# A two-layer convolution kernel: the ScalarE order of the filter pass changed, and the statistics of its output taken on ScalarE by sums of value and square instead of by VectorE's batch-norm instructions

## What is computed

```
# layer 0: four levels; level i works on x pooled by 2**i
y = relu(conv3x3(pool(x, 2**i), ds_w3[i], dilation d_i)); y = conv1x1(y, ds_w1[i])
# attention on each level: the first 16 channels
ker = gelu(mean(f_att) @ kg_w1.T + kg_b1) @ kg_w2.T + kg_b2      # one 3x3 kernel per image and channel
out = conv1x1(concat(conv13x13(f_att) + depthwise3x3(f_att, ker), f_idt))
x   = x + conv1x1(sum over levels of the upsampled outputs)
# layer 1: the group norm needs mean and variance of the x that layer 0 gave
x   = x + sum over ten branches of (5x5 convolution, nine shifts of a 3x3 convolution) of group_norm(x)
```

## Time and profile before

| what | value |
| --- | --- |
| median of 3 runs | 3051.51 us (3051.09 to 3056.02) |
| the profiled execution's own time | 3052.12 us |
| its span in the profile | 3050.3 us |
| TensorE matmuls busy in the span | 2688.6 us (88%) |
| VectorE busy | 2153.3 us (71%) |
| ScalarE busy | 992.0 us (33%) |
| GpSimd busy | 645.2 us (21%) |

### The profile page before, as it was taken

One profiled execution on the slowest core, in us unless ns is written; L12 is line 12 of the kernel. 1 busy time (PEld: TensorE's weight loads), 2 busy tenths in 40 slices (PEclk: granted clock), 3 DMA queues, 4 the chain that ended last, 5 costly groups with the idle time before them and its releaser, 6 DMA issues. The chain is left out here.

```text
span 3050.3 us, 39267 instructions
## 1 busy us (share of the span) xinstructions
PE 2688.6 (88%) x12262; PEld 2153.5 (71%) x12262; DVE 2153.3 (71%) x3003; ACT 992.0 (33%) x1606; POOL 645.2 (21%) x732
## 2 busy tenths in 40 slices
PE   0499999996999699999999688888994999999998
PEld 0366776664788678888888566777773777777776
DVE  7444444433345488888888778888876999999998
ACT  1011111110111077778777422222211333232332
POOL 5444433331222143443344200000001000000000
PEclk9999999998889699999999799999996999999999
DMA  4422222210000299999998313333344223333332
GB/s 75 100 71 70 65 71 64 65 42 16 8 13 15 39 199 212 218 215 214 212 217 208 112 59 140 143 127 127 129 151 161 88 88 117 92 113 97 109 103 69
DMA packets 288699, 337.99 MB, mean 111 GB/s; under 512 B 24816, under 2 KB 243824, under 8 KB 274288
## 3 DMA queue, kind: packets, MB, share of 16 engines
q1 hardware_dynamic: 285072, 336.15, 41.2%
q10 hardware_dynamic: 3552, 0.89, 0.1%
HBM read 211.60 MB, written 122.62 MB: 110 GB/s over the span
## 5 line engine op out<-in xcount | busy, mean ns | idle before, releaser
L373 PE MATMUL ps_all<-vh,u_h 128*128 128x512 f32 x960 | 384.7, 401 | 28.7 <-DVE vl L2633 27.8
L375 PE MATMUL ps_all<-vh,u_l 128*128 128x512 f32 x960 | 383.3, 399 | 0.0
L374 PE MATMUL ps_all<-vl,u_h 128*128 128x512 f32 x960 | 382.9, 399 | 0.0
L2542 ACT ACTIVATE vh<-rt,gn 128x528 fp32r<-128x528 f32 x192 | 130.4, 727 | 445.9 <-DVE rt L2610 331.2
L373 PE MATMUL ps_all<-vh,t_h 128*128 128x512 f32 x576 | 231.2, 401 | 22.3 <-DVE vl L1691 22.3
L373 PEld LDWEIGHTS ps_all<-vh,u_h 128*128 128x128 f32 x960 | 180.9, 188 | 82.3 <-issue 35.7
L375 PE MATMUL ps_all<-vh,t_l 128*128 128x512 f32 x576 | 229.7, 399 | 0.0
L374 PE MATMUL ps_all<-vl,t_h 128*128 128x512 f32 x576 | 229.4, 398 | 0.0
L375 PEld LDWEIGHTS ps_all<-vh,u_l 128*128 128x128 f32 x960 | 181.0, 189 | 46.2
L374 PEld LDWEIGHTS ps_all<-vl,u_h 128*128 128x128 f32 x960 | 181.1, 189 | 45.5
L373 PE MATMUL ps_all<-nh,w3h 128*128 128x512 f32 (+1 forms) x396 | 161.0, 407 | 32.3 <-POOL nl L1078 24.5
(11 more groups left out here) (384 smaller groups left out, 6688.6 us busy)
## 6 DMA issues: line engine op xcount, KB each, us to landing
xc<-in_x SPq DMA_DIRECT2D x128, 256.0 KB, 3.8
xr<-in_x SPq DMA_DIRECT2D x128, 256.0 KB, 4.2
x_layer<-xr SPq DMA_DIRECT2D x64, 512.0 KB, 2.7
xq<-x_layer SPq DMA_DIRECT2D x32, 1024.0 KB, 4.8
x_layer<-xq SPq DMA_DIRECT2D x32, 1024.0 KB, 3.8
out<-ot SPq DMA_DIRECT2D x64, 512.0 KB, 5.2
xw<-in_x SPq DMA_DIRECT2D x112, 288.0 KB, 5.0
xw<-x_layer SPq DMA_DIRECT2D x16, 1152.0 KB, 8.7
```

Of the source, the lines that this page charges most:

```text
L373: pe.matmul(o, wh, xh, start=first, stop=False, skip_group_check=True)
L374: pe.matmul(o, wh, xl, start=False, stop=False, skip_group_check=True)
L375: return pe.matmul(o, wl, xh, start=False, stop=last, skip_group_check=True)
L2542: act.activation(vh[:, v % 2, n, :, :].rearrange("p a b -> p (a b)"), rt[:, n, :, :].rearrange("p a b -> p (a b)"), ACT.Identity, scale=gn ...
```

## The change

In the convolution pass ScalarE gets one more activation per tile, `low_phases`, which lays out the low part for the phases 0 and 1 in a new buffer `rp_l`; the products for `dc` 2 and 3 read their low part there, without a step. It waits for VectorE's `r_low`; TensorE waits for it ahead of the third product. The added pads of `rp_l` are two more memsets on GpSimd, once.

In the filter pass `bn_stats` is gone from `add_attention`. ScalarE's new `moments(a, c)` has four activations of 1024 elements per partition per chunk: for each half of the chunk a sum of the values and a sum of the squares of value minus the image's earlier mean, written to a scratch area (`void`, in the place of the weights `kg2`) that nothing reads; each waits for the one before it. `collect` becomes six small VectorE operations in a row in place of one. The copy of bank 0 for t = 2 stood first in the next period; it now stands in the image's own period, ahead of `high_dynamic(n, 2)`. SyncE's `store_x` waits for the chunk's moments before it lets the buffer be loaded again.

```diff
 # convolution pass, ScalarE
+                    def low_phases(i, t):
+                        n = NT * i + t
+                        act.wait_ge(r_l, 1 + n + 1)
+                        v = rl[:, t % 2, :, 2:2 + W].bitcast(F32).rearrange("p n (q d) -> p n q d", d=4)[:, :, :, 0:2]
+                        act.activation(rp_l[:, t % 2, :, :, 1:33].rearrange("p d n q -> p n q d"), v,
+                                       ACT.Identity).then_inc(r_p, 1)
...
                                 high_phases(*later(i, t, 1))
+                                low_phases(*later(i, t, 1))
                             features(i, t)
 # convolution pass, TensorE
                         for dc in range(4):
+                            if dc == 2:
+                                pe.wait_ge(r_p, n + 1)
...
+                            low = rl[u] if dc < 2 else rp_l[v]
                             mm = product(pe, ps_fa[:, 0:272].rearrange("p (n q) -> p n q", q=34), fa_h[:, dc, :],
-                                         fa_l[:, dc, :], rp_h[v], rl[u], dc == 0, dc == 3)
+                                         fa_l[:, dc, :], rp_h[v], low, dc == 0, dc == 3)
 # filter pass, SyncE, store_x
                         sp.wait_ge(x_st, 16 * (4 * a + c + 1))
                         alone(sp)
+                        sp.wait_ge(bn, 4 * (4 * a + c + 1))
+                        alone(sp)
 # filter pass, ScalarE
+                    def moments(a, c):
+                        act.wait_ge(qfree, 4 + 16 * a + 4 * c + 4)
+                        for h in range(2):
+                            v = xq[:, c % 2, 8 * h:8 * h + 8, :].rearrange("p a b -> p (a b)")
+                            k = 2 * c + h
+                            act.wait_ge(bn, 16 * a + 2 * k)
+                            act.activation(void, v, ACT.Identity, accum_out=sx[:, k:k + 1]).then_inc(bn, 1)
+                            act.wait_ge(bn, 16 * a + 2 * k + 1)
+                            alone(act)
+                            act.activation(void, v, ACT.Square, bias=nm0[:, bass.ds(a, 1)],
+                                           accum_out=sq[:, k:k + 1]).then_inc(bn, 1)
...
                     def period(i, a, s, n):
                         first = i is None
-                        if a is not None:
-                            copy(a, 2)
                         if i is not None:
                             high(i, 8, isinstance(i, int) and i == 0)
...
                             high_lk(a, 1)
+                            moments(a, 0)
...
                             high_lk(a, 3)
+                            moments(a, 1)
                         if i is not None:
                             copy(i, 1)
                         if n is not None:
                             high_dynamic(n, 1, first)
                             high(n, 6, first)
+                        if a is not None:
+                            moments(a, 2)
+                        if n is not None:
                             high(n, 7, first)
+                        if i is not None:
+                            copy(i, 2)
+                        if n is not None:
                             high_dynamic(n, 2, first)
+                        if a is not None:
+                            moments(a, 3)
 # filter pass, VectorE
-                        for e in range(4):
-                            dve.bn_stats(stat[:, 4 * c + e, :], xq[:, c % 2, 4 * e:4 * e + 4, :].rearrange(
-                                "p a b -> p (a b)")).then_inc(bn, 1)
...
-                        stats.done(dve.bn_aggr(mv, stat[:, :, :].rearrange("p a b -> p (a b)")))
+                        mo.done(dve.tensor_reduce(tx, sx[:, :], AX.X, ALU.add))
+                        mo.done(dve.tensor_reduce(tq, sq[:, :], AX.X, ALU.add))
+                        mo.wait(dve)
+                        mo.done(dve.tensor_scalar(mv[:, 0:1], tx, one, None, ALU.mult))
+                        mo.wait(dve)
+                        alone(dve)
+                        mo.done(dve.tensor_tensor(dd, mv[:, 0:1], nm0[:, bass.ds(s, 1)], ALU.add))
+                        mo.wait(dve)
+                        alone(dve)
+                        mo.done(dve.tensor_tensor(dd, dd, dd, ALU.mult))
+                        mo.wait(dve)
+                        stats.done(dve.scalar_tensor_tensor(mv[:, 1:2], tq, one, dd, ALU.mult, ALU.subtract))
```

More of the change, by code:

```diff
@@ L132, in conv_kernel @@
         kb1 = mb("kb1", [ATT // 2, 1])
-        kg2 = mb("kg2", [ATT // 2, 9, P])
+        kg2a = mb("kg2", [P, 9, P])
+        kg2 = kg2a[0:ATT // 2, :, :]
         kb2 = mb("kb2", [P, 9])
@@ L1438, in conv_kernel @@
             rp_h = sb("rp_h", [P, 2, 4, 8, 36], F32R, stack=st)
+            rp_l = sb("rp_l", [P, 2, 2, 8, 36], F32R, stack=st)
             ft = sb("ft", [P, 4, NPAIR, 9], stack=st)
@@ L1450, in conv_kernel @@
             main, m_c, y_d = sa("main"), sa("m_c"), sa("y_d")
-            r_f, r_h, r_l = sa("r_f"), sa("r_h"), sa("r_l")
+            r_f, r_h, r_l, r_p = sa("r_f"), sa("r_h"), sa("r_l"), sa("r_p")
             q_f, q_x = sa("q_f"), sa("q_x")
@@ L1458, in conv_kernel @@
             w_t3 = Steps(sa("w_t3"), 10)
-            NT3, NFA, NPD = 7, 13, 8
+            NT3, NFA, NPD = 7, 13, 10
             def later(i, t, k):
@@ L1550, in pads @@
                             pool.memset(t[:, :, :, 0:W + 2:W + 1].bitcast(F32), 0.0).then_inc(w_z, 1)
-                        for t in (rp_h,):
+                        for t in (rp_h, rp_l):
                             v = t[:, :, :, :, :].rearrange("p s d n q -> p (s d n) q").bitcast(F32)
@@ L1666, in _ @@
                     high_phases(0, 0)
+                    low_phases(0, 0)
                     with act.Fori(0, B - 1) as i:
@@ L1850, in conv_kernel @@
             ms = sb("ms", [P, 2], stack=st)
+            nm0 = sb("nm0", [P, B], stack=st)
+            sx = sb("sx", [P, 8], stack=st)
+            sq = sb("sq", [P, 8], stack=st)
+            void = kg2a[:, :, :].rearrange("p a b -> p (a b)")[:, 0:8 * W]
+            mo = Steps(sl("mo"), 5)
+            nm_s = sl("nm_s")
             b_p, b_w, b_h, b_g = sl("b_p"), sl("b_w"), sl("b_h"), Steps(sl("b_g"), 20)
@@ L2052, in _ @@
                     act.wait_ge(b_p, 4)
+                    act.wait_ge(nm_s, 1)
+                    act.wait_ge(t_c, 3)
                     schedule(act, period)
@@ L2186, in collect @@
                         stats.start(s)
-                        stats.done(dve.bn_aggr(mv, stat[:, :, :].rearrange("p a b -> p (a b)")))
+                        mo.start(s)
+                        one = 1.0 / (NPAIR * W)
+                        tx, tq, dd = small[:, 6:7], small[:, 7:8], small[:, 8:9]
+                        mo.done(dve.tensor_reduce(tx, sx[:, :], AX.X, ALU.add))
[10 more added lines that the diff above has]
+                        stats.done(dve.scalar_tensor_tensor(mv[:, 1:2], tq, one, dd, ALU.mult, ALU.subtract))
                     def spread(s):
@@ L2299, in period @@
                             low_dynamic(n, 2)
+                    dve.tensor_scalar(nm0[:, :], gn0[:, :, 0], -1.0, None, ALU.mult).then_inc(nm_s, 1)
                     t_r.start(0)
```

## The result

The changed kernel took 3071.36 us (median of 4 runs, 3071.09 to 3074.81), the kernel before 3052.66 us on the same chip: a ratio of 1.0059 [1.0047, 1.0072], 18.7 us slower. The forecast was 3076 us, and slower with a chance of 0.81. The span of the profiled execution is 3069.3 us, against 3050.3.

The account below looks back on a forecast made before the run. TensorE bounds the convolution pass; in the filter pass it has some 82 us open, with waits for bank 0's copy. -12.8 + 12.2 + 4.5 + 11.3 + 9.5 = +24.7 us, so 3076 against 3051.5; range 3057 to 3093.

Parts of the forecast that it names:

- convolution pass: TensorE there: two of a tile's four stepped matmuls go, 0.10 us each over 64 tiles, a gain of 12.8 us.
- component 6, i = 1 to 6: Filter pass: the stop ahead of component 6 becomes 7.4 us six times, 44.4 against 32.2, +12.2 us.
- component 6, i = 7: Filter pass, i = 7: a new stop of 3.1 us ahead of component 6, with 1.45 of clock, +4.5.
- group mean for component 0: Stops move from component 0 to the group mean: 5.1 us four times, 3.8 twice, 28.0 against 16.7, +11.3.
- clock: TensorE's slower clock after stops: six losses of 2.55 us for four of 1.45, +9.5; another 1.45 at i = 7.
- Chunk 1 stands between `high_lk(a, 3)` and `copy(i, 1)`: ScalarE, filter pass: this `moments` call of 5.05 us lengthens the stop ahead of component 6 to 7.4 us, six times.
- Chunk 3 stands ... ahead of `high(i, 8)`: ScalarE, period's end: this `moments` call delays `collect`; the group mean waits 5.1 us four times and 3.8 twice.
- the relief of VectorE decides: Rival, copy ahead of component 6: chunk 1's moments end before component 5, stops 2.4 us, -56, so 2995 us; chance 0.05.
- only component 6 suffers: Rival: chunk 3's moments and `collect` end within component 0's 5.03 us; -18.6, so 3033 us; chance 0.07.
- the one without a gain in the convolution pass: Rival: DMA or ScalarE takes TensorE's place as bound in the convolution pass, which gives nothing; 3089 us; chance 0.13.
- ScalarE and the rest: nothing: Convolution pass: `low_phases` takes 1.1 us of ScalarE's 2.00 us idle per tile; no cost counted there or for DMA.
- The table load: ScalarE, ahead of the loop period's first activation: 1.28 us by the row; the skill's 2.66 would add 5.5 us.

Follow-up runs that it names:

- the sixth experiment: The changed kernel with one call moved: `moments(a, 1)` behind `copy(i, 1)` in place of ahead of it; 3033.27 us, ratio 0.9929 to the kernel before.
- the seventh: The changed kernel with VectorE's `collect(s)` ahead of `low(i, 8)`, so not waiting for the table load and `high(i, 8)`; 3049.7 us, ratio 0.9991 to the kernel before.
- the first experiment: The kernel before with only the convolution pass's part of the change (`low_phases`, its buffer and its wait); 3044.96 us, ratio 0.9967.

## Why the prediction was right

| term | forecast, us | measured, us |
| --- | --- | --- |
| convolution pass | -12.8 | -9.6 |
| component 6, i = 1 to 6 (32.2 before) | +12.2 | +12.4 (8.30, then 7.23 to 7.30; sum 44.6) |
| component 6, i = 7 | +3.1 | +2.9 |
| group mean for component 0 (16.7 before) | +11.3 | +11.4 (5.24, 5.21 three times, 3.60, 3.63; sum 28.1) |
| clock | +9.5 + 1.45 | +1.5 |
| tail behind component 8 of i = 7 | 0 | -0.8 (52.2 to 51.4) |
| not forecast | | +1.2 |
| sum | +24.7 | +19.0 |

The measured sum is that of the spans. What was not forecast is 0.65 us less at attention 1 of i = 1, and 1.9 us more in earlier and later stages, which the change does not touch.

**The mechanism held, to 0.2 us in each stop but one.** The one is component 6 at i = 1, 8.30 us where 7.4 was forecast; the five others are each 0.1 to 0.2 us shorter than forecast, so that the sum is met to 0.2 us by luck. "Chunk 1 stands between `high_lk(a, 3)` and `copy(i, 1)`": the sixth experiment takes away that alone and gets 38 us back. "Chunk 3 stands ... ahead of `high(i, 8)`": the seventh cuts that chain behind the call and gets 21.7 back. The rivals in which the relief of VectorE decides, or only component 6 suffers, are out by the rows above, and the one without a gain in the convolution pass by the first experiment.

**The mis-sized term is the clock.** The forecast took 2.55 us for a long stop and 1.45 for one of 2.9, for each alike, and nothing for 1.6. Worked out as above, the kernel before lost 15.9 us behind its six long stops (2.4 to 2.8 each), 7.9 behind the four of 2.9 (2.0 each, not 1.45) and 1.1 behind the two of 1.6, where the granted clock does not fall (1.00 in the earlier trace rows). The changed kernel lost 12.3 behind its six stops at component 6, 13.4 behind the six at the group mean (2.6, 1.7, 3.0, 2.5, 1.9, 1.7) and nothing measurable at i = 7. That is 25.7 against 24.9: +0.8, and 1.5 by the busy time of the windows, where +10.95 was forecast. The loss of 3.2 us in the convolution pass hid a part of this miss in the sum. Two things were missed: that a longer stop ahead of component 6 costs no more clock and sometimes less, and that the loss behind the earlier trace rows's 2.93 us goes on beyond the eight matmuls that were read. Equal stops differ too. Windows of the kernel after, over the first 4.9 us of component 6, both behind a stop of 7.2 us:

```profile
1976.09:1981.00 4.91, 4.91 (x12) 3.84 (x13) 4.46 (x7) 0.94 (x2) 0.00 (x0) 0.50 0.76 240
2053.07:2058.00 4.93, 4.93 (x15) 3.97 (x16) 4.47 (x7) 0.94 (x2) 0.00 (x0) 0.70 0.75 239
```

The granted clock stays at 0.50, the 1.2 GHz level, for all of the first and for a part of the second. What decides between them no run here settles. The filter pass of the first experiment is that of the kernel before and has the same stops, but there those of 4.9 to 5.0 us lose 1.7 and those of 2.93 us 3.3, where the kernel before lost 2.4 to 2.8 and 2.0. Windows of the first experiment, from a component 6 behind 4.96 us and a component 0 behind 2.93:

```profile
1900.21:1904.90 4.69, 4.69 (x14) 3.72 (x15) 4.44 (x7) 0.41 (x1) 0.00 (x0) 0.64 0.78 252
1925.18:1932.00 6.82, 6.82 (x17) 5.37 (x18) 3.83 (x6) 1.79 (x2) 0.00 (x0) 0.55 0.65 239
```

The longer stop costs less here. So a price for a stop that is read from one execution does not hold for the same stop in another.

**The convolution pass gained 9.6 in place of 12.8**, just below the bounds of 10 to 17. By the windows TensorE's busy time fell by 11.1 us and 1.5 us of new idle time came. The changed product is as forecast: the low part now takes the pitch of the others (1311.59 to 1311.72, 0.13 us against 0.23 in the earlier trace rows). Timeline of TensorE after:

```profile
1311.46 0.29 PE L374 MATMUL ps_all<-rp_h,fa_h 128*128 128x272 f32 x1
1311.59 0.29 PE L375 MATMUL ps_all<-rp_l,fa_h 128*128 128x272 f32 x1
1311.72 0.29 PE L376 MATMUL ps_all<-rp_h,fa_l 128*128 128x272 f32 x1
```

A tile without a stop takes 9.60 or 9.63 us in place of 9.81 and 9.87, 0.22 us less: 14 us in all, more than forecast. But nine of 63 take 9.7 to 10.3 and give 3.3 us back, and the last 18 matmuls take 4.87 us in place of 3.71, as the granted clock is 0.65 there and was 1.00. In the nine VectorE's `vl`, the low part of the next tile's input, comes late. Timelines of GpSimd, VectorE, ScalarE and TensorE ahead of the slowest one:

```profile
1127.02 3.03 POOL L1545 TENSOR_TENSOR xr<-xr,zr 128x1024 f32<-128x1024 f32 x1
...
1128.28 2.85 DVE L1727 TENSOR_TENSOR rl<-rf,rh 128x1024 fp32r<-128x1024 f32 x1 [0.26 <-ACT rh L1619]
...
1131.16 1.17 ACT L1637 ACTIVATE rp_l<-rl 128x512 fp32r<-128x512 f32 x1 [0.90 <-DVE rl L1727]
...
1135.40 2.16 POOL L1545 TENSOR_TENSOR xr<-xr,zr 128x1024 f32<-128x1024 f32 x1
...
1135.53 2.59 DVE L1702 TENSOR_TENSOR vl<-cr,vh 128x512 fp32r<-128x512 f32 x1
...
1138.25 0.49 PE L374 MATMUL ps_all<-vh,t_h 128*128 128x512 f32 x1 [0.46 <-DVE vl L1702]
```

The late `rl` does not stop TensorE here; it holds `low_phases`, and with it ScalarE, back by 0.90 us. TensorE stops for the late `vl`, 0.16 to 0.46 us in five of the nine tiles. "ScalarE and the rest: nothing" therefore held for ScalarE in most tiles (1.20 us for `low_phases`, 1.02 to 1.08 us of its pause left of the 2.00 in the earlier trace rows) and for DMA, but not for VectorE beside GpSimd, which the forecast did not look at. Without the additions the pass gains 14.5. GpSimd's first addition ends at 1130.05, VectorE's `rl` at 1131.13, 1.08 us behind it. The Trainium skill, page "SBUF — State Buffer", section "Who interferes with whom", says that a VectorE instruction with two inputs in SBUF contends with a GpSimd instruction that reads SBUF, and calls the port pair that they share an exclusive lock. The trace agrees: 1130.05 plus the undisturbed 1.22 us is 1131.27, against the measured end at 1131.13, and 1137.56 plus 0.68 is 1138.24 for `vl`, against 1138.12. All 56 `vl` and `rl` of the pass that are over 0.15 us too long end so, 0.13 or 0.14 us ahead of the end of GpSimd's addition plus their undisturbed time.

**The table load** was put at 1.28 us by the row, and the row after says the same: 2004.74 to 2006.03. The 2.66 us that the Trainium skill gives on its page "ScalarE: Activation LUTs", section "What ACT_TABLE_LOAD costs", would have made the four loop stops at the group mean 6.6 us, an estimate; they are 5.2.

**Busy times.** ScalarE's grew by 206 us (220 forecast). VectorE's fell by 45.5 us, not 80: in the filter pass by 72, but in the convolution pass it rose by 26, as its instructions are stretched beside GpSimd's; without the additions it is busy for 466 us there, against 542 and 516.

## What to carry to other kernels

On an engine that keeps a written order, what a new piece of work costs is set by what stands behind it: with the same 32 calls of about 5 us each, and the convolution part in both, the kernel is 19 us slower than before in one order and 79 us faster in another. Put such work right behind the releases that the bound engine waits for, and before a move follow the chain to the next wait, since a stop that goes uncovers the one behind it. Moving work from a loaded engine to an idle one was worth its price only then: 48 us here, for 79 us of `bn_stats` taken off VectorE.

## What the runs showed of the hardware that was not expected

- The clock loss behind a stop of TensorE is no function of its length alone. It was 0.35 to 0.4 us behind most stops of 2.0 to 2.6 us, but 1.6 behind four of five with 2.3 us in the sixth experiment; 2.0 behind 2.93 us in the kernel before and 3.3 in the first experiment; 1.7 to 1.9 behind 3.5 to 3.6 us; 1.4 to 2.8 behind 7.2 us.
- A VectorE subtraction of 1.22 us took up to 2.95 us, and one of 0.68 us up to 2.68, where GpSimd was adding at the same time: it did not slow down in part, but ended its own length, less 0.13 us, behind GpSimd's end, in all 56 cases of the convolution pass.
- Behind a matmul of 272 columns that reads its moving data with a step of four elements the next one starts 0.10 us later than behind one with neighbouring elements (0.23 against 0.13 us), on both sides of the change.
